# Degree sums of a hypergraph layer on ScalarE, the router's weights side by side, and two combine additions on GpSimd

## The reference

```
H   = (adj != 0)                                    # 512 x 512, per graph
Be  = 1 / H.sum(axis=1)                             # the degrees: nodes in each hyperedge
Dn  = 1 / (H @ adj[0])
conv(x, W) = Dn * (H @ (Be * (H.T @ (x @ W.T)))) + b
x1  = x + conv(layer_norm(relu(conv(norm(x), W1))), W2) + norm(x)
x2  = norm(x1)
logits = x2 @ router_w + router_b                   # 4 experts
mask   = softmax over the top 2 of the logits, 0 elsewhere
comb   = sum over e of mask[e] * silu(x2 @ expert_w[e] + expert_b[e])
out    = x1 + rms_norm(x2 + comb @ out_w + out_b) * norm_w
```

## Time and profile before

| what | value |
|---|---|
| median of 3 runs | 738.5 us (737.72 to 739.07) |
| the profiled execution, its own time | 737.89 us |
| span of that execution | 736.4 us, so 1.5 us lie outside the span |
| granted TensorE clock, mean | 0.987 |
| PE, DVE, ACT, POOL busy | 95%, 87%, 67%, 41% of the span |

### The profile page before, as it was taken

How to read it: one execution, slowest core, us unless ns; L and a number is a source line. 1 busy time by engine, 2 the same in 40 slices (tenths; PEclk the granted TensorE clock), 3 DMA queues, 4 the chain that set the end, 5 groups by cost and what they waited for, 6 DMA issues and landing times.

```text
span 736.4 us, 16435 instructions
## 1 busy us (share of the span) xinstructions
PE 697.6 (95%) x5573; PEld 486.5 (66%) x5573; DVE 637.7 (87%) x1569; ACT 495.6 (67%) x971; POOL 298.5 (41%) x685
## 2 busy tenths in 40 slices
PE   4787999999999999999999999999999999999983
PEld 2365595866758586776858577685957668595772
DVE  3887799889989898998989999898998989898676
ACT  4565858667595857668594866859486685957563
POOL 4142524245352524435352434436243543624233
PEclk9999999999999999999999999999999999999997
DMA  8447449376665839476573947556493756537312
GB/s 285 181 76 240 99 131 229 59 232 134 214 129 151 200 58 267 103 219 123 167 175 73 273 81 228 114 194 148 101 259 67 234 116 202 110 89 161 58 31 57
DMA packets 42591, 111.73 MB, mean 152 GB/s; under 512 B 4160, under 2 KB 5312, under 8 KB 42560
## 3 DMA queue, kind: packets, MB, share of 16 engines
q0 software_dynamic: 13536, 41.42, 31.8%
q1 hardware_dynamic: 29024, 69.92, 27.3%
HBM read 69.91 MB, written 16.25 MB: 117 GB/s over the span
## 4 chain that ended last, share of the span: by engine, by line
PE 86%; DVE 6%; ACT 3%; DMA 1%; issue 1%; POOL 1%; SPq 0%; POOLq 0%; DVEq 0%; ACTq 0%
PE bank L1278 16%; PE bank L1279 16%; PE bank L1280 16%; PE bank L1363 7%; PE bank L1364 7%; PE bank L1422 4%; PE bank L1423 4%; PE bank L1392 3%; PE bank L1332 3%; PE bank L1394 3%; PE bank L1380 2%; PE bank L1325 2%; DMA b1b<-b 1%; PE bank L1435 1%; PE bank L1410 1%
## 5 line engine op out<-in xcount | busy, mean ns | idle before, releaser
L1278 PE MATMUL bank<-xth,ewh 128*128 128x512 f16 (+1 forms) x272 | 101.0, 371 | 2.5 <-DVE ewl L794 2.5
L1279 PE MATMUL bank<-xtl,ewh 128*128 128x512 f16 (+1 forms) x272 | 101.0, 371 | 0.0
L1280 PE MATMUL bank<-xth,ewl 128*128 128x512 f16 (+1 forms) x272 | 100.8, 371 | 0.0
L519 ACT ACTIVATE silu<-bank,ebcol,ksc 128x512 f32<-128x512 f32 x120 | 90.5, 769 | 9.2 <-POOL comb L389 4.9
L1278 PE MATMUL bank<-w2h,hnth 128*128 128x256 f16 x256 | 70.3, 275 | 0.2 <-issue 0.2
L1279 PE MATMUL bank<-w2l,hnth 128*128 128x256 f16 x256 | 70.3, 275 | 0.0
L1280 PE MATMUL bank<-w2h,hntl 128*128 128x256 f16 x256 | 70.2, 274 | 0.0
L560 ACT ACTIVATE a1h<-bank,be 128x256 f16<-128x256 f32 x64 | 26.9, 470 | 55.7 <-PE bank L1423 52.5
L893 DVE SCALAR_TENSOR_TENSOR hntl<-bank,hnth 128x512 f16<-128x512 f32 x64 | 42.7, 687 | 23.5 <-ACT hnth L537 23.5
L666 ACT ACTIVATE uh<-bank,be 128x256 f16<-128x256 f32 x64 | 26.9, 471 | 53.7 <-PE bank L1364 53.7
L1422 PE MATMUL bank<-xsh,h 128*128 128x256 f16 x256 | 59.3, 280 | 1.1 <-DVE xsl L776 1.1
(11 more groups left out here) (260 smaller groups left out, 2124.9 us busy)
## 6 DMA issues: line engine op xcount, KB each, us to landing
adjin<-adj SPq DMA_DIRECT2D x16, 1024.0 KB, 5.3
adjtin<-adjt SPq DMA_DIRECT2D x16, 1024.0 KB, 7.9
xin<-x SPq DMA_DIRECT2D x16, 512.0 KB, 7.0
xb<-xn SPq DMA_DIRECT2D x16, 512.0 KB, 4.0
xb<-x POOLq DMA_DIRECT2D x16, 512.0 KB, 8.7
xb<-b POOLq DMA_DIRECT2D x16, 512.0 KB, 5.4
xb<-vadd POOLq DMA_DIRECT2D x16, 512.0 KB, 4.5
out<-x SPq DMA_DIRECT2D x15, 512.0 KB, 4.9
```

Source lines behind the costliest of these rows:

```text
L519: af(silu[:, i % 4, :], bank[E_BANK[i]][:, :], ACT.Silu, bias=ebcol[:, i:i + 1], scale=ksc[:, 2:3]).then_inc(silu_dn, 1)
L1278: mm(outp, lh, rh, start=first, stop=False)
L1279: mm(outp, lh, rl, start=False, stop=False)
L1280: return mm(outp, ll, rh, start=False, stop=last)
```

## The change

Five edits:

1. The 16 degree matmuls and their bank columns go. ScalarE sums the rows of `ht16` of the next graph instead: `count_edges`, four ACTIVATEs of 512 elements with a row sum (`accum_out`), put at the end of its body, behind `squares`. `degrees` on VectorE now waits for the fourth of them. `be` gets two buffers. For graph 0 VectorE makes `ht16` in four pieces with a row sum each (`first_ht`), and `degrees` follows it.
2. `rwh` and `rwl` lie side by side in `rw16`: one matmul of 8 columns gives high by high and high by low; one of 4 columns adds low by high. So 16 matmuls instead of 24 per graph. VectorE adds the two column groups with one more small instruction (`lga`). The router in the tail stays as it was.
3. `a2_half` does its four matmuls with `a1h` first, and waits for `a1l` only for the other four. `turned_x2` 0 moves between them.
4. `dna` and `dnb` are computed on GpSimd (`scale_dn`), behind the two output DMA issues.
5. The additions of experts 1 and 2 run on GpSimd (`add_up`), the second behind the DMA issue of `add_b2`; VectorE adds expert 3 alone.

The diff, cut to its core:

```
+            def scale_dn(g):
+                gp.wait_ge(d_step, 4 * g + 4)
+                tt(dna[:, :], dn[:, :], ksc[:, 0:1].to_broadcast([P, CT]), ALU.mult).then_inc(dn_scaled, 1)
+                tt(dnb[:, :], dn[:, :], ksc[:, 1:2].to_broadcast([P, CT]), ALU.mult).then_inc(dn_scaled, 1)
...
-            def add_half(f):
-                gp.wait_ge(comb_st, 7 * f + 2)
-                tt(comb[:, :, :], comb[:, :, :], silu[:, 2:4, :], ALU.add).then_inc(half_sum, 1)
+            def add_up(f, e):
+                gp.wait_ge(comb_st, 7 * f + e + 1)
+                if e == 2:
+                    gp.wait_ge(half_sum, 2 * f + 1)
+                tt(comb[:, :, :], comb[:, :, :], silu[:, 2 * (e % 2):2 * (e % 2) + 2, :], ALU.add).then_inc(half_sum, 1)
...
                 if i >= 6:
-                    act.wait_ge(half_sum, f + 1)
+                    act.wait_ge(half_sum, 2 * f + 1)
...
+            def count_edges(act, g, odd):
+                act.wait_ge(ht_made, g + 5)
+                act.wait_ge(deg_dn, 4 * g)
+                act.wait_ge(be_dn, g + 1)
+                for t in range(CT):
+                    af(counted[:, t, :], ht16[odd][:, t, :], ACT.Copy, accum_out=deg[:, t:t + 1]).then_inc(deg_dn, 1)
...
                 if ffn and prep:
                     squares(act, f, 0)
                     squares(act, f, 1)
+                if prep:
+                    count_edges(act, g, 1 - odd)
...
+            def first_ht():
+                dve.wait_ge(adjt_in, 16)
+                for t in range(CT):
+                    TS(ht16[0][:, t, :], adjtin[:, t, :], 0.0, None, ALU.not_equal, ALU.add,
+                       accum_out=deg[:, t:t + 1]).then_inc(ht_made, 1)
+                dve.wait_ge(ht_made, CT)
...
-            def combine_sum(f, e):
-                if e == 2:
-                    dve.wait_ge(half_sum, f + 1)
-                dve.wait_ge(comb_st, 7 * f + 2 * e - 1)
-                for s in ((slice(0, C),) if e == 2 else (slice(0, C // 2), slice(C // 2, C))):
-                    TT(comb[:, :, s], comb[:, :, s], silu[:, 2 * (e % 2):2 * (e % 2) + 2, s], ALU.add).then_inc(comb_st, 1)
+            def combine_sum(f):
+                dve.wait_ge(half_sum, 2 * f + 2)
+                dve.wait_ge(comb_st, 7 * f + 4)
+                for j in range(2):
+                    s = slice(256 * j, 256 * j + 256)
+                    TT(comb[:, :, s], comb[:, :, s], silu[:, 2:4, s], ALU.add).then_inc(comb_st, 1 + j)
...
-                STT(lg[:, :, :], bank[R_BANK][:, 0:CT * NE].rearrange("p (t e) -> p t e", e=NE), ksc[:, 4:5],
-                    rbb[:, :, :], ALU.mult, ALU.add).then_inc(lg_dn, 1)
+                raw = bank[R_BANK][:, 0:CT * 2 * NE].rearrange("p (t e) -> p t e", e=2 * NE)
+                STT(lga[:, :, :], raw[:, :, NE:2 * NE], ksc[:, 4:5], rbb[:, :, :], ALU.mult, ALU.add).then_inc(lga_dn, 1)
+                dve.wait_ge(lga_dn, f + 1)
+                STT(lg[:, :, :], raw[:, :, 0:NE], ksc[:, 4:5], lga[:, :, :], ALU.mult, ALU.add).then_inc(lg_dn, 1)
...
+            def degrees(g, odd):
+
+                dve.wait_ge(deg_dn, 4 * g)
+                TS(dmax[:, :], deg[:, :], 1.0, None, ALU.max).then_inc(be_max, 1)
                 dve.wait_ge(be_max, g + 1)
-                v.reciprocal(be[:, :], dmax[:, :]).then_inc(be_dn, 1)
+                v.reciprocal(be[odd][:, :], dmax[:, :]).then_inc(be_dn, 1)
...
+                pe.wait_ge(a1_hi, 4 * g + CG * half + CG)
                 if half == 0 and ffn:
                     pe.wait_ge(u_lo, 4 * g)
                     pe.wait_ge(x1_dn, 4 * (g - 1) + 2)
...
+                part(a1h, True, False)
+                if ffn and half == 0:
+                    turned_x2(g - 1, 0)
+                pe.wait_ge(a1_lo, 4 * g + CG * half + CG)
+                part(a1l, False, True)
...
-                    for e in range(CT):
-                        for k in range(CT):
-                            ins = mm(bank[DEG_BANK][:, DEG][:, e:e + 1], h16[:, k, P * e:P * e + P], one16[:, :],
-                                     start=(k == 0), stop=(k == CT - 1))
-                    ins.then_inc(deg_rdy, 1)
...
-                            ins = three(bank[R_BANK][:, NE * t:NE * t + NE], xth[:, k, P * t:P * t + P],
-                                        xtl[:, k, P * t:P * t + P], rwh[:, k, :], rwl[:, k, :], k == 0, k == KD - 1)
+                            b = bank[R_BANK][:, 2 * NE * t:2 * NE * t + 2 * NE]
+                            mm(b, xth[:, k, P * t:P * t + P], rw16[:, k, :], start=(k == 0), stop=False)
+                            ins = mm(b[:, 0:NE], xtl[:, k, P * t:P * t + P], rwh[:, k, :], start=False, stop=(k == KD - 1))
```

More of the change, by code:

```diff
@@ L128, in build @@
         xb = sb("xb", [P, CT, D], F32)
-        dmax, be = (sb(n, [P, CT], F32) for n in ("dmax", "be"))
+        counted = sb("counted", [P, CT, C], F16)
+        deg, dmax = sb("deg", [P, CT], F32), sb("dmax", [P, CT], F32)
+        be = (sb("be_even", [P, CT], F32), sb("be_odd", [P, CT], F32))
         dsum, dclip, drec, dn, dna, dnb = (sb(n, [P, CT], F32) for n in ("dsum", "dclip", "drec", "dn", "dna", "dnb"))
@@ L151, in build @@
         spare, spare_p = sb("spare", [P, 1], F32), sb("spare_p", [P, 1], F32)
-        lg = sb("lg", [P, CT, NE], F32)
+        lg, lga = sb("lg", [P, CT, NE], F32), sb("lga", [P, CT, NE], F32)
         ldf, tie, beat = (sb(n, [P, CT, NE, NE], F32) for n in ("ldf", "tie", "beat"))
@@ L397, in body @@
                         add_yf(q, j)
+                if conv:
+                    if not ffn:
+                        gp.wait_ge(b_scale, 1)
+                    scale_dn(g)
                 if prep and ffn:
@@ L912, in y_part, with a1_part @@
                     ALU.mult, ALU.add).then_inc(y_dn, 1)
-            def a1_part(g, j):
+            def a1_part(g, odd, j):
                 dve.wait_ge(a1_hi, 4 * g + CG * j + CG)
                 for e in range(CG * j, CG * j + CG):
-                    STT(a1l[:, e, :], bank[A1_BANK[j]][:, D * (e % CG):D * (e % CG) + D], be[:, e:e + 1], a1h[:, e, :],
+                    STT(a1l[:, e, :], bank[A1_BANK[j]][:, D * (e % CG):D * (e % CG) + D], be[odd][:, e:e + 1], a1h[:, e, :],
                         ALU.mult, ALU.subtract).then_inc(a1_lo, 1)
@@ L1014, in body @@
                     x1_half(f, 1, late)
-                if conv:
-                    degrees(g)
+                if conv and ffn:
+                    degrees(g, odd)
                 if ffn:
@@ L1085, in body @@
                     h_aggr(g, 1)
-                    TS(dnb[:, :], dn[:, :], ksc[:, 1:2], None, ALU.mult).then_inc(d_step, 1)
                     if not ffn:
@@ L1384, in a2_half, with part @@
             def a2_half(g, odd, half, ffn):
-                pe.wait_ge(a1_lo, 4 * g + CG * half + CG)
+                def part(a, first, last):
+                    for d in range(KD):
+                        for k in range(CG * half, CG * half + CG):
+                            ins = mm(bank[A2_BANK[d]][:, :], a[:, k, P * d:P * d + P], ht16[odd][:, k, :],
+                                     start=(first and k == 0), stop=(last and k == CT - 1))
+                        if last and half == 1:
+                            ins.then_inc(a2_rdy, 1)
+                pe.wait_ge(a1_hi, 4 * g + CG * half + CG)
                 if half == 0 and ffn:
@@ L1389, in a2_half @@
                     pe.wait_ge(x1_dn, 4 * (g - 1) + 2)
-                for d in range(KD):
-                    for k in range(CG * half, CG * half + CG):
-                        mm(bank[A2_BANK[d]][:, :], a1h[:, k, P * d:P * d + P], ht16[odd][:, k, :],
-                           start=(k == 0), stop=False)
-                        ins = mm(bank[A2_BANK[d]][:, :], a1l[:, k, P * d:P * d + P], ht16[odd][:, k, :],
-                                 start=False, stop=(k == CT - 1))
-                    if half == 1:
-                        ins.then_inc(a2_rdy, 1)
+                part(a1h, True, False)
[3 more added lines that the diff above has]
+                part(a1l, False, True)
             def body(pe, g, odd, conv, ffn, late, prep):
```

72 lines of the change are left out of this document (35 added, 37 removed).

## The result

The changed kernel takes 729.09 us (median of 4 runs, 727.4 to 731.03) against 738.17 for the kernel before in the same job: a ratio of 0.9866, 95% interval 0.9835 to 0.9898, or 9.1 us less. The forecast was 732.5 with a range from 729.8 to 737.2.

What follows compares the result with a forecast made beforehand. TensorE was taken as the bound, one side chain close behind: 0.60 us saved less a 0.17 wait gives 0.43 in 13 bodies, 5.6, plus 0.4 in graph 15: 6.0, so 738.5 becomes 732.5; range 729.8 to 737.2.

Steps and rivals of the forecast that it cites:

- TensorE is the bound, and its work sets the gain: TensorE never waits in steady bodies; dropping degree matmuls saves 0.40 us and router matmuls 0.20, together 0.60 per graph.
- Shift of the chain up to silu 6 "about 0": From the counts through z, roots and GpSimd's first addition to silu 6: -0.14 + 0.12 us, net about 0.
- Counts at 0.65, ending at 359.84 + 2.68: ScalarE's four counts behind the squares: 0.65 us from start to start, ending at 362.5.
- A wait of 0.17 per graph: At `out_product` 0 TensorE would be ready at 393.14 and wait for `ctl` until about 393.31.
- rival 1: Full gain: counts cost 0.60 or less, the chain stays ahead, 14 x 0.60 = 8.4 us, so 730.1; chance 0.16.
- The sign set for being wrong: The prediction's working is wrong if the wait falls at the router or second transposes, or bodies reach 41.88 us.
- The slack of 0.11 at `out_product` 0 is that of the long chain: `ctl` is ready 0.11 us before TensorE needs it, behind one chain: squares, `be`, z, roots, additions, silu, last product, sum.
- Last product 0.37 earlier once the addition is gone: On VectorE, the combine's last product starts when silu 7 ends, at 388.61 instead of 389.03: 0.37 us earlier.
- Second addition covered by 0.6: GpSimd's second addition, behind the DMA issue, ends at 390.4, 0.6 us before VectorE's sum of expert 3 at 391.04.
- Rival 4: Counts on ScalarE become the bound; slower from a count of 0.79 us; at 1.08 each, 754; chance 0.06.
- Rival 5: GpSimd's second addition holds VectorE's last product until 390.4, each body 1.4 us longer, some 756; chance 0.03.
- Graphs 0, 1 and 15: Outside the 13 bodies: graph 0 gives 0, give or take 0.4 us, graph 1 nothing, graph 15 0.4.

Runs made afterwards that it cites:

- degrees alone: The kernel before with only the degrees moved to ScalarE counts, with two `be` buffers and `first_ht`: 732.72 us, ratio 0.9926.
- router and addition: The kernel before with only the router's product changed and the second addition moved to GpSimd: 735.56 us, ratio 0.9942.
- order undone: The changed kernel with the old order in A2: transposes of x2 first, then high and low parts in turn, behind `a1l`: 729.9 us, ratio 0.9856.
- dna undone: The changed kernel with `dna` and `dnb` back on VectorE: 731.43 us, ratio 0.9877.
- one count more: The changed kernel with one more unused ScalarE sum over 512 entries ahead of the four counts: 731.81 us, ratio 0.9887.
- Addition alone: The kernel before with only the second addition moved from VectorE to GpSimd: 738.94 us, ratio 1.0002.
- the two count experiments: The changed kernel with one or two more unused ScalarE sums over 512 entries ahead of the four counts: 731.81 and 742.4 us.

## Why the prediction was right and wrong

- *TensorE is the bound, and its work sets the gain*: right. 0.40 for the degrees and 0.20 for the router were exact (degrees alone 0.400; router and addition 0.204). 0.04 for the reorder was missing (order undone). Together they are the 0.64.
- *Shift of the chain up to silu 6 "about 0"*: **this is the step that failed, a mis-sized term of the sum.** It was -0.35 (387.11 and 382.72 against the zero), and -0.40 at silu 7's end. The prediction added -0.14 (`a1h`), -0.14 (`dna`), 0 (`dnb`) and +0.26 (`lga`). The traces give -0.41 at `a2l`, before the router (371.24 before, 366.79 after, against the zero), +0.26 for `lga`, and -0.20 for `dna` and `dnb` together (the 0.19 of dna undone, to 0.01). So 0.27 of the miss is the front of the chain, which came earlier by all that TensorE gained on A1, and 0.06 is `dna` with `dnb`.
- *Counts at 0.65, ending at 359.84 + 2.68*: this is why the front was mis-sized. The price is 0.61, and the first starts 0.10 before the read's end, not 0.02 behind it. Against the zero the counts end at 358.25 - 356.83 = 1.42 instead of 1.65, so `be` was not late: `a1h` waited for A1 and not, as forecast, for `be`, and came 0.37 earlier (363.21 - 360.87 against 358.80 - 356.83) instead of 0.14. That this start is carried down the chain is shown by one count more: with the counts 0.61 later, `a1h` is 0.59 and the last product 0.56 later against the zero. The Trainium skill (ScalarE: Activation LUTs, What ACT_TABLE_LOAD costs) gives an ACTIVATE with immediate scale and bias 186 + 0.833 N ns, by which 512 columns would take 613 ns, an estimate. The rows' 0.61 agree; the Trainium skill has no time for the accumulator read.
- *A wait of 0.17 per graph*: none came. With the term at -0.40 the predicted chain itself would have had `ctl` 0.77 earlier, against TensorE's 0.60 less 0.11 of slack: no wait, and 730.3 by the prediction's own sum (13 x 0.60 + 0.4). That is rival 1 (730.1), given 0.16, with its condition (counts at 0.60 or less) missed by 0.01. From there to 729.09 the reorder gives 13 x 0.04 = 0.5, the kernel before measured 738.17 beside the change where the sum began from 738.5, and some 0.3 lie outside the 13 bodies. The sign set for being wrong, bodies that reach 41.88, was met: 41.84.
- *The slack of 0.11 at `out_product` 0 is that of the long chain*: wrong in kind, a second error. It is that of a short chain through TensorE's own transposes, and moves with whatever shortens TensorE. The long chain met it at `hntl` 2, within 0.03. Addition alone shows it: product 0.39 earlier, `ctl` 0.00. By itself this error was small. With both chains but the predicted shift, VectorE would have been free for `hntl` 2 at 388.61 + 0.03 + 1.14 = 389.78 (in times of before) and wanted at 390.20 - 0.60 = 389.60; 0.18 late, less the 0.05 that `out_product` 0 can give (half of its 0.11, as the prediction took it), is a wait of 0.13, an estimate, where 0.17 was forecast.
- *Last product 0.37 earlier once the addition is gone*: right (0.39). *Second addition covered by 0.6*: right in effect, 0.73; it takes 2.66, over the 2.4 that the prediction allowed, and starts before the DMA issue has ended.
- *Rival 4, slower from a count of 0.79*: that counts can become the bound is shown, but by another way than the prediction's: TensorE then stops at the transposes of x2. By the two count experiments 0.33 are spare and 0.64 is the gain, so four counts may be 0.97 longer in sum: (0.97 / 4) + 0.61 = 0.85 each.
- *Rival 5, GpSimd holds VectorE*: in no run. The last product takes 1.22 beside the second addition and took 1.21 before. The additions and VectorE's sums never overlap, so what the Trainium skill (SBUF — State Buffer, on the shared port pair) says of two SBUF inputs is not shown here.
- *Graphs 0, 1 and 15*: 0.4 in all against 9.1 - 8.4 = 0.7 measured. With tails of the same kernel 2.3 us apart, and its D of graph 2 at 109.29 in one run and 110.33 in the other, how that splits stays open.

## What to carry to other kernels

A small slack at a wait tells how late the last link is, not which chain owns it: follow it back past each meeting point, and see whether it ends in the bound engine itself, for then it moves along. Near a balance, edits do not add up: the same router edit was worth +0.16 us a body alone and -0.20 beside another that was worth nothing alone. Price each edit for both the bound engine and the chain next to it. To give a chain's spare time a number, lengthen it on purpose, and then look where the bound engine stops: a lengthened step may feed another chain too, as the counts here feed x2.

## What the runs showed of the hardware that was not expected

- A sum on ScalarE is two records, an ACTIVATE of 0.61 (512 columns) and a read of 0.19, but costs only 0.61 from start to start: the next ACTIVATE begins 0.09 to 0.10 before the read ends (356.32 against 356.22 + 0.19).
- Four fp32 transposes take 0.47 behind 4-column matmuls (order undone) and 0.43 behind 512-column ones (the change), at a clock of 1.00 in both.
- A wait between 256-column matmuls leaves hardly a mark in TensorE's busy time: a body with waits of 0.25 and 0.11 is busy for 42.57 of 42.65.
- The granted clock late in the program differs between runs of one kernel (a mean of 0.86 or 1.00 over the same 12.5 us). The tail differed by 2.3 us with it, which blurs effects of 0.2%; how much of the 2.3 the clock itself makes is not shown. The length of a body did not move (41.840 in both).
